# Attention in plain fp32 instead of rounded high and low parts, with scores on 64-row halves and weighted sums on 64-column halves

## The chip, the cores and the metric

The kernel runs on one core of one Trainium2 chip. The metric is the device time of the whole program in microseconds (us), the median of the runs.

## What is computed

The reference is a network of two layers on 4096 tokens (2 sequences of 2048) of 256 features: a Mamba block, a tree of gated feed-forward nodes, an attention, and a feed-forward layer of 64 experts of which each token takes 8. The change touches the attention alone:

```python
q = (hidden_states @ Wq).reshape(b, s, H, D).transpose(0, 2, 1, 3)   # H = 16, D = 64
k = (hidden_states @ Wk).reshape(b, s, HKV, D).transpose(0, 2, 1, 3) # HKV = 4
v = (hidden_states @ Wv).reshape(b, s, HKV, D).transpose(0, 2, 1, 3)
q = _apply_rope(q, cos, sin)
k = _apply_rope(k, cos, sin)
scores = jnp.einsum('bkgqd,bkpd->bkgqp', qg, k) * scale
scores = jnp.where(causal, scores, jnp.float32(-1e+30))
probs = jax.nn.softmax(scores, axis=-1)
out = jnp.einsum('bkgqp,bkpd->bkgqd', probs, v).reshape(b, H, s, D)
return out @ Wo
```

## The kernel before

The stages run one after the other: Mamba (lines 56 on), the tree, the projection with rotation, the attention (lines 1318 to 1793), routing with the output projection, the experts, and the sum. The projection multiplies its plain fp32 weights and inputs at line 1229, for 8 chunks of 512 tokens, 5 pairs, 2 parities and 2 blocks of features: 160 matmuls.

The attention goes through 32 heads (2 sequences of 16). Groups of 4 heads share keys and values, so there are 8 groups. The 2048 queries of a head are 4 bands of 512, each of 4 tiles of 128. A unit is a long and a short band, (3, 0) or (2, 1), and a head is 2 units. In a unit, `CHUNKS` lists 20 score chunks (tile j of band s against keys c of 512 columns; the last chunk of a tile is 1 to 4 blocks of 128 wide, since the attention is causal), and `GROUPS` lists 20 groups (band s against block kb of 128 keys). `STEPS` is 20. One unit's scores are made while the unit before it is turned and summed.

The arithmetic is done in a rounded fp32 format (`F32R`) with high and low parts. `qbuf` holds a query's high part in rows 0 to 63 and its low part in rows 64 to 127; `kbuf` holds the keys' high and low parts, twice over the rows, in two slots for two groups. A score chunk is thus two matmuls over 128 rows (line 1514), and on the diagonal a third adds the mask (line 1518). VectorE takes the maximum (line 1719), ScalarE the exponential (line 1671, bias at line 1732's result). TensorE turns 4 blocks of 128x128 of a group into `ps_t`, which has two banks (line 1527; fewer on the diagonal: 3, 2 and 1). ScalarE copies them as high part (line 1679) and VectorE takes the low part by a subtraction (line 1739). `weigh` (line 1539) multiplies the values, whose high and low columns stand side by side in `vbuf`, with each part: two matmuls into `ps_o`. At a band's end ScalarE copies `ps_o` to `folding` (line 1685), `fold` adds its halves and turns it back, 4 small plain fp32 matmuls (line 1550), and VectorE normalises (line 1757).

TensorE's order is written out by hand: in step v come the scores of the next unit (from step 1 to 17), the turning of group v, and the weighted sum of group v - 2; at a unit's end come the last two sums, the last scores and the fold. `RING` = 5 banks hold scores, `SLOTS` = 4 hold turned groups.

POOL rounds the queries of the next head and makes their low parts (lines 1622, 1624), and once a group does the same for keys (1604, 1606) and values (1612, 1614, 1630). SP issues the loads of queries, keys and values, the stores of the output (line 1494), and the small loads of constants at the start (line 1460); ahead of the first scores TensorE waits for keys and queries.

In the Mamba stage, line 285 sums states (plain fp32, 128 rows), line 277 spreads a row (rounded fp32, 112 rows) and line 265 multiplies with 16 rows (plain fp32). Lines 2112 and 2114, in the routing, multiply plain fp32 with 64 rows.

## Time and profile before

| | us |
|---|---|
| median of 3 runs | 4915.38 |
| lowest and highest run | 4910.9, 4915.8 |
| span of the profiled execution | 4914.1 |
| of it TensorE busy | 4375.7 |

The page gives no time of the profiled execution beside its span; 4914.1 us lies within the three runs, 1.3 us under their median. "Busy" is the union of an engine's instructions. Matmuls are recorded with modelled ends that reach over the start of the next one, so the busy time of a matmul is more than what it takes from the engine; the distance between starts is not subject to this. PE is the matmul side of TensorE, PEld its weight load. A releaser behind an arrow is the instruction that ended a wait.

### The profile page before, as it was taken

To read this page: it belongs to the slowest core of one execution; us is meant where nothing else is said; L and a number is where in the kernel's file an instruction comes from. 1 tells how busy PE (TensorE), PEld (TensorE's weight loads), DVE (VectorE), ACT (ScalarE), POOL (GpSimd) and SP (SyncE) were. 2 spreads that over 40 slices of the span, in tenths; PEclk is the share of its full clock that TensorE was granted. 3 is DMA by queue.
4 is the path that set the end of the run, shared out by engine and by line. 5 is a ranking of instruction groups with operands and counts; after the bars stand their busy time and mean duration, and the time that the engine had idled before them with its cause. 6 is when DMAs were issued, how large, how long until landed. Compare 5 with 4: busy or idle time off the path is not lost. (4 is left out here: it accounts for less than half of the span.)

```text
span 4914.1 us, 82249 instructions
## 1 busy us (share of the span) xinstructions
PE 4375.7 (89%) x20280; PEld 3077.8 (63%) x20311; DVE 3433.2 (70%) x7334; ACT 2814.4 (57%) x6629; POOL 1757.2 (36%) x1411
## 2 busy tenths in 40 slices
PE   7888888789999979999999999999966549999996
PEld 3333333356666568888888888888855437777775
DVE  7999999934434878888888888888844443333336
ACT  7777777522221068888888888888833224444441
POOL 5989989700100021212121221212135553333330
PEclk8999999999999989999999999999987769999999
DMA  1000000021102530202112021202044425554548
GB/s 44 13 13 13 13 27 9 9 87 57 47 17 82 178 102 26 53 26 52 42 44 53 26 52 28 58 26 53 26 155 143 143 97 155 155 157 152 157 138 344
DMA packets 305965, 377.40 MB, mean 77 GB/s; under 512 B 123200, under 2 KB 236608, under 8 KB 300240
## 3 DMA queue, kind: packets, MB, share of 16 engines
q1 hardware_dynamic: 232784, 257.37, 17.3%
q0 software_dynamic: 26112, 73.44, 4.2%
q10 hardware_dynamic: 46944, 45.16, 3.4%
q8 instruction: 50, 0.82, 0.1%
q14 instruction: 75, 0.61, 0.0%
HBM read 223.07 MB, written 152.76 MB: 76 GB/s over the span
## 5 line engine op out<-in xcount | busy, mean ns | idle before, releaser
L1739 DVE TENSOR_TENSOR probsT<-ps_t,probsT 128x512 fp32r<-128x512 f32 (+3 forms) x1280 | 779.5, 609 | 137.8 <-ACT probsT L1679 116.2
L1679 ACT ACTIVATE probsT<-ps_t 128x512 fp32r<-128x512 f32 (+3 forms) x1280 | 686.6, 536 | 256.1 <-PE ps_t L1527 231.3
L1671 ACT ACTIVATE probs<-ps_s,negm 128x512 f32<-128x512 f32 (+3 forms) x1297 | 812.5, 627 | 28.1 <-DVE negm L1732 27.1
L1539 PE MATMUL ps_o<-probsT,vbuf 128*128 128x512 f32 (+3 forms) x2560 | 815.8, 402 | 6.8 <-ACT folding L1685 6.3
L1514 PE MATMUL ps_s<-kbuf,qbuf 128*128 (+1 forms) x2602 | 768.7, 380 | 57.8 <-ACT probs L1671 31.5
L1719 DVE TENSOR_REDUCE pmax<-ps_s 128x1 f32<-128x512 f32 (+3 forms) x1301 | 777.6, 600 | 47.3 <-PE ps_s L1514 23.0
L1527 PE MATMUL ps_t<-idn,probs 128*128 128x128 f32 x4352 | 694.8, 275 | 13.8 <-DVE probsT L1739 13.8
L527 POOL TENSOR_TENSOR dBx<-u,b_all 128x1024 f32<-128x1024 f32 x255 | 612.4, 2414 | 96.5 <-DVE h L623 66.8
L1527 PEld LDWEIGHTS ps_t<-idn,probs 128*128 128x128 f32 x4352 | 517.3, 141 | 135.3 <-DVE probsT L1739 40.9
L1514 PEld LDWEIGHTS ps_s<-kbuf,qbuf 128*128 128x128 f32 x2602 | 445.3, 189 | 177.9 <-issue 63.9
L1622 POOL CAST qbuf<-room_a 128x512 fp32r<-128x512 f32 x132 | 83.1, 630 | 1264.6 <-DMA room_a<-q_scr 754.1
L285 PE MATMUL ps_y<-hc,idn 128*128 128x512 f32 x1024 | 500.5, 612 | 31.3 <-POOL hc L535 29.7
L428 ACT ACTIVATE ps_a<-delta,neg_a 128x512 f32<-128x512 f32 x512 | 350.8, 690 | 226.7 <-DVE h L623 225.3
L623 DVE TENSOR_TENSOR_SCAN h<-ps_a,h_in,dBx 128x512 f32<-128x512 f32 x384 | 469.3, 1266 | 0.9 <-POOL hc L535 0.7
L2588 POOL DMA_INDIRECT y<-y,place x288 | 276.7, 961 | 490.4 <-DVE y L2625 476.4
L2497 PE MATMUL ps_gu<-room_a,xT 128*128 x1160 | 423.3, 488 | 0.3 <-ACT xT L2550 0.3
L1539 PEld LDWEIGHTS ps_o<-probsT,vbuf 128*128 128x128 f32 x2560 | 392.3, 191 | 34.3 <-ACT folding L1685 22.0
L2621 DVE TENSOR_TENSOR hid<-ps_gu,sg 128x192 f32<-128x192 f32 x290 | 103.7, 358 | 402.6 <-ACT sg L2554 374.3
L285 PEld LDWEIGHTS ps_y<-hc,idn 128*128 128x128 f32 x1024 | 197.4, 195 | 216.3 <-issue 153.4
L2190 POOL DMA_INDIRECT xs<-xe,dest x256 | 246.8, 964 | 206.6 <-issue 206.3
L2511 PE MATMUL ps_y<-room_a,hT 96*128 x1152 | 296.4, 379 | 0.0
L632 DVE TENSOR_TENSOR hc<-h,ps_c 128x1024 f32<-128x1024 f32 x224 | 273.3, 1220 | 23.3 <-PE ps_c L277 5.6
(275 smaller groups left out, 6982.7 us busy)
## 6 DMA issues: line engine op xcount, KB each, us to landing
room_b<-xs ACTq DMA_DIRECT2D x294, 136.0 KB
room_a<-q_scr SPq DMA_DIRECT2D x528, 64.0 KB
room_c<-y SPq DMA_DIRECT2D x32, 1024.0 KB, 8.2
room_a<-W_guT SPq DMA_DIRECT2D x64, 384.0 KB
q_scr<-rot SPq DMA_DIRECT2D x64, 256.0 KB, 2.9
attn<-ostage SPq DMA_DIRECT2D x128, 128.0 KB
at<-attn SPq DMA_DIRECT2D x32, 512.0 KB
room_a<-W_downT SPq DMA_DIRECT2D x64, 192.0 KB
```

The costliest lines, as they stand in the source:

```text
L285: last = nc.tensor.matmul(ps_y[:, i, :], idn[:, :], hc[:, q % 2, i, :], start=n == 0, stop=n == NST - 1)
L428: nc.scalar.activation(ps_a[:, s % RING, :], delta[:, c % 2, d, :], ACT.Exp, scale=neg_a[:, d, n:n + 1]).then_inc(dA_ready.sem, 1)
L527: nc.gpsimd.tensor_tensor(dBx[:, q % DRIVES, :, :], u[:, hv * DH:(hv + 1) * DH, :], b_all[:, n:n + 1, :].to_broadcast((P, DH, TC)), ALU.mu ...
L623: nc.vector.tensor_tensor_scan(h[:, q % 2, i, :], ps_a[:, s % RING, :], dBx[:, q % DRIVES, i, :], 0.0 if first else h_in[:, n, d:d + 1], A ...
L1514: last = nc.tensor.matmul(ps_s[:, u % RING, 0:w], qbuf[:, BAND * s + j, :], kbuf[:, bass.ds(kslot, 1), part, c * CW:c * CW + w], start=par ...
L1527: last = nc.tensor.transpose(ps_t[:, t % 2, j * P:(j + 1) * P], probs[:, k, place(k, s, j, kb), :], idn[:, :])
L1539: last = nc.tensor.matmul(ps_o[:, lo:], vbuf[:, kb, :, :], probsT[:, g % SLOTS, part, lo:], start=kb == 0 and part == 0, stop=kb == BAND * ...
L1671: nc.scalar.activation(probs[:, k, at:at + n, :], ps_s[:, u % RING, 0:n * P], ACT.Exp, bias=negm[:, tile, :], accum_out=sums[:, s, j, c:c ...
L1679: nc.scalar.activation(probsT[:, g % SLOTS, 0, lo:], ps_t[:, t % 2, lo:], ACT.Copy).then_inc(high_t.sem, 1)
L1719: nc.vector.reduce_max(pmax[:, tile, c:c + 1], ps_s[:, u % RING, 0:blocks(s, j, c) * P], axis=mybir.AxisListType.X).then_inc(cmax.sem, 1)
L1739: nc.vector.tensor_tensor(probsT[:, g % SLOTS, 1, lo:], ps_t[:, t % 2, lo:], probsT[:, g % SLOTS, 0, lo:].bitcast(F32), ALU.subtract).then ...
L2497: last = nc.tensor.matmul(ps_gu[:, b, 0:2 * FF], xT[:, b, k, :], w_gu[:, bass.ds(e % WSLOTS, 1), k, :], start=k == 0, stop=k == KD - 1)
```

## The change

The operands `qbuf`, `kbuf`, `vbuf` and `probsT` become plain fp32 with no parts. `kbuf` has one slot instead of two, and POOL fills it chunk by chunk at a group's end, each chunk after its last use by the old group. Both row halves of `qbuf` and `kbuf` hold the same 64 rows; a score chunk is one matmul that uses rows 0 to 63 or 64 to 127 in turn, and the mask is added by two bf16 matmuls on the same rows. A weighted sum is one matmul whose 64 output columns go to the lower or the upper half of `ps_o` by the parity of kb; where kb = 1 doesn't cover the first columns, a matmul with zeros fills them. The sums are issued in pairs in every odd step. The turned groups are copied once, by ScalarE in even and by VectorE in odd steps (`by_act`), and the semaphore `t_out` is split into one for each engine. `SLOTS` is 5.

```diff
-    SLOTS = 4
+    SLOTS = 5
...
-    LAG = 2
...
+    K_USED = [max(k * STEPS + v + 1 for k in range(NU) for v, (s, j, chunk_no) in enumerate(CHUNKS[k]) if chunk_no == c) for c in range(BANDS)]
+    K_ORDER = sorted(range(BANDS), key=lambda c: K_USED[c])
...
+    def by_act(g):
+
+        return g % 2 == 0
...
-        idn_r = sb("idn_r", [P, P], F32R)
         idn_2 = sb("idn_2", [P, HD])
-        mask = sb("mask", [P, P])
-        mask_r = sb("mask_r", [P, P], F32R)
-
-        qbuf = sb("qbuf", [P, QT, P], F32R)
-        kbuf = sb("kbuf", [P, 2, 2, LENGTH], F32R)
-        vnext = sb("vnext", [P, QT, 2, HD], F32R)
-        vbuf = sb("vbuf", [P, QT, 2, HD], F32R)
+        halves = sb("halves", [P, 2, P])
+        mask = sb("mask", [P, 2, P])
+        halves_b = sb("halves_b", [P, 2, P], BF16)
+        mask_b = sb("mask_b", [P, 2, P], BF16)
+        nothing = sb("nothing", [P, HD])
+
+        qbuf = sb("qbuf", [P, QT, P])
+        kbuf = sb("kbuf", [P, LENGTH])
+        vbuf = sb("vbuf", [P, QT, HD])
         probs = sb("probs", [P, NU, BLOCKS, P])
-        probsT = sb("probsT", [P, SLOTS, 2, CW], F32R)
...
         @block.tensor
         def _(pe):
-            def scores(hx, kslot, k, v):
+            def scores(hx, k, v):
                 s, j, c = CHUNKS[k][v]
                 u = k * STEPS + v
                 w = blocks(s, j, c) * P
+                rows = slice(HD * (u % 2), HD * (u % 2 + 1))
                 pe.wait_ge(exp_done.sem, exp_done.at(hx, u - RING + 1))
-                for part in range(2):
-                    last = nc.tensor.matmul(ps_s[:, u % RING, 0:w], qbuf[:, BAND * s + j, :],
-                                            kbuf[:, bass.ds(kslot, 1), part, c * CW:c * CW + w],
-                                            start=part == 0, stop=part == 1 and c < s)
+                last = nc.tensor.matmul(ps_s[:, u % RING, 0:w], qbuf[rows, BAND * s + j, :],
+                                        kbuf[rows, c * CW:c * CW + w], start=True, stop=c < s)
                 if c == s:
-                    last = nc.tensor.matmul(ps_s[:, u % RING, w - P:w], idn_r[:, :], mask_r[:, :], start=False, stop=True)
+                    for part in range(2):
+                        last = nc.tensor.matmul(ps_s[:, u % RING, w - P:w], halves_b[rows, part, :], mask_b[rows, part, :],
+                                                start=False, stop=part == 1)
                 last.then_inc(s_done.sem, 1)
 
             def turn(hx, k, g):
                 s, kb = GROUPS[k][g]
                 t = use(k, g)
                 pe.wait_ge(exp_done.sem, exp_done.at(hx, band_end(k, s)))
-                pe.wait_ge(t_out.sem, t_out.at(hx, t - 1))
+                bank_free(pe, hx, t)
                 for j in range(max(0, kb - BAND * s), BAND):
                     last = nc.tensor.transpose(ps_t[:, t % 2, j * P:(j + 1) * P], probs[:, k, place(k, s, j, kb), :], idn[:, :])
                 last.then_inc(t_done.sem, 1)
...
             def weigh(hx, group, k, g):
                 s, kb = GROUPS[k][g]
                 lo = max(0, kb - BAND * s) * P
-                pe.wait_ge(t_out.sem, t_out.at(hx, use(k, g) + 1))
+                rows = slice(HD * (kb % 2), HD * (kb % 2 + 1))
+                taken(pe, hx, use(k, g))
                 if kb == 0:
                     pe.wait_ge(o_ev.sem, o_ev.at(hx, 2 * k + (s == UNITS[k][1])))
                 if kb % BAND == 0:
                     pe.wait_ge(v_set.sem, v_set.at(group, V_ORDER.index(kb // BAND) + 1))
-                for part in range(2):
-                    last = nc.tensor.matmul(ps_o[:, lo:], vbuf[:, kb, :, :],
-                                            probsT[:, g % SLOTS, part, lo:],
-                                            start=kb == 0 and part == 0, stop=kb == BAND * s + BAND - 1 and part == 1)
-                last.then_inc(pv_done.sem, 1)
+                if kb == 1 and lo:
+                    nc.tensor.matmul(ps_o[rows, 0:lo], nothing[:, :], probsT[:, g % SLOTS, lo:2 * lo], start=True, stop=False)
+                nc.tensor.matmul(ps_o[rows, lo:], vbuf[:, kb, :], probsT[:, g % SLOTS, lo:],
+                                 start=kb == 0 or kb == 1 and not lo, stop=kb >= BAND * s + BAND - 2).then_inc(pv_done.sem, 1)
 
             def fold(hx, k, short):
 
                 t = fold_use(k, short)
                 pe.wait_ge(o_ev.sem, o_ev.at(hx, 2 * k + short + 1))
-                pe.wait_ge(t_out.sem, t_out.at(hx, t - 1))
+                bank_free(pe, hx, t)
                 for j in range(BAND):
                     last = nc.tensor.matmul(ps_t[:, t % 2, j * HD:(j + 1) * HD], folding[:, j * P:(j + 1) * P], idn_2[:, :],
                                             start=True, stop=True)
                 last.then_inc(f_done.sem, 1)
 
             pe.wait_ge(rounded.sem, 2)
+            pe.wait_ge(nothing_set.sem, 1)
             s_done.credit(pe)
             t_done.credit(pe)
             pv_done.credit(pe)
             f_done.credit(pe)
-            pe.wait_ge(k_ready.sem, 1)
+            pe.wait_ge(k_ready.sem, BANDS)
             pe.wait_ge(q_ready.sem, 2)
             for v in range(LEAD + 1):
                 if v == STEPS:
                     pe.wait_ge(q_ready.sem, BANDS)
-                scores(0, 0, *chunk(0, v, 0)[1:])
+                scores(0, *chunk(0, v, 0)[1:])
             with pe.Fori(0, NHEADS) as hx:
                 group = pe.snap(hx // GROUP)
-                slot = pe.snap(group % 2)
-                slot_next = pe.snap(((hx + 1) // GROUP) % 2)
+                group_next = pe.snap((hx + 1) // GROUP)
                 for k in range(NU):
                     def next_scores(v):
                         heads, unit, number = chunk(k, v, LEAD)
                         if number == 0 and unit == 0:
                             pe.wait_ge(q_ready.sem, q_ready.at(hx + 1, 2))
-                            pe.wait_ge(k_ready.sem, (hx + 1) // GROUP + 1)
                         elif number == 0:
                             pe.wait_ge(q_ready.sem, q_ready.at(hx + heads, 4))
-                        scores(hx + heads, slot_next if heads else slot, unit, number)
+                        if heads and unit == 0 and number < BANDS:
+                            pe.wait_ge(k_ready.sem, k_ready.at(group_next, K_ORDER.index(number) + 1))
+                        scores(hx + heads, unit, number)
 
                     for v in range(STEPS):
                         if 0 < v < LATE:
                             next_scores(v)
                         turn(hx, k, v)
-                        if v >= LAG:
-                            weigh(hx, group, k, v - LAG)
+                        if v % 2 and v > 1:
+                            weigh(hx, group, k, v - 3)
+                            weigh(hx, group, k, v - 2)
                         if v == FOLD[k]:
                             fold(hx, k, 0)
+                    next_scores(LATE)
+                    next_scores(LATE + 1)
                     weigh(hx, group, k, STEPS - 2)
-                    next_scores(LATE)
                     weigh(hx, group, k, STEPS - 1)
-                    for v in range(LATE + 1, STEPS + 1):
-                        next_scores(v)
+                    next_scores(STEPS)
                     fold(hx, k, 1)
...
+            def set_keys(g, c):
+
+                nc.gpsimd.tensor_copy(kbuf[:, c * CW:(c + 1) * CW], kstage[:, c * CW:(c + 1) * CW]).then_inc(k_ready.sem, 1)
...
             def queries(hx, n):
-                j, low = QUEUE[n], slice(HD, P)
-                tiles = slice(BAND * j, BAND * (j + 1))
-                after(q_ld[j].sem, q_ld[j].at(hx))
-                nc.gpsimd.tensor_copy(qbuf[:, tiles, :], qstage[:, tiles, :]).then_inc(high_q.sem, 1)
-                after(high_q.sem, high_q.at(hx, n + 1))
-                nc.gpsimd.tensor_tensor(qbuf[low, tiles, :], qstage[low, tiles, :], qbuf[low, tiles, :].bitcast(F32),
-                                        ALU.subtract).then_inc(q_ready.sem, 1)
-                after(q_ready.sem, q_ready.at(hx, n + 1))
+                tiles = slice(BAND * QUEUE[n], BAND * (QUEUE[n] + 1))
+                after(q_ld[QUEUE[n]].sem, q_ld[QUEUE[n]].at(hx))
+                nc.gpsimd.tensor_copy(qbuf[:, tiles, :], qstage[:, tiles, :]).then_inc(q_ready.sem, 1)
 
             def set_values(g, n):
                 b = slice(BAND * V_ORDER[n], BAND * (V_ORDER[n] + 1))
-                nc.gpsimd.tensor_copy(vbuf[:, b, :, :], vnext[:, b, :, :].bitcast(F32)).then_inc(v_set.sem, 1)
+                nc.gpsimd.tensor_copy(vbuf[:, b, :], vstage[:, b, :]).then_inc(v_set.sem, 1)
...
             with pool.Fori(0, NGROUPS) as g:
-                head_queries(g * GROUP)
-                keys(g + 1)
-                after(v_set.sem, v_set.at(g))
-                values(g + 1)
-                with pool.Fori(1, GROUP) as j4:
+                with pool.Fori(0, GROUP - 1) as j4:
                     head_queries(pool.snap(g * GROUP + j4))
-
+                head = pool.snap(g * GROUP + GROUP - 1)
+                after(s_done.sem, s_done.at(head, STEPS))
+                for n in range(2):
+                    queries(head + 1, n)
+                after(k_ld.sem, k_ld.at(g + 1))
+                for c in K_ORDER:
+                    after(s_done.sem, s_done.at(head, K_USED[c]))
+                    set_keys(g + 1, c)
+                for n in range(2, BANDS):
+                    queries(head + 1, n)
+
+                after(v_ld.sem, v_ld.at(g + 1))
                 for n, used in enumerate(V_USED):
                     after(pv_done.sem, pv_done.at(g * GROUP + GROUP - 1, used))
                     set_values(g + 1, n)
...
-            def high(hx, k, g):
+            def take_turned(hx, k, g):
                 s, kb = GROUPS[k][g]
                 t, lo = use(k, g), max(0, kb - BAND * s) * P
                 act.wait_ge(t_done.sem, t_done.at(hx, k * STEPS + g + 1))
                 act.wait_ge(pv_done.sem, pv_done.at(hx, k * STEPS + g - SLOTS + 1))
-                nc.scalar.activation(probsT[:, g % SLOTS, 0, lo:], ps_t[:, t % 2, lo:], ACT.Copy).then_inc(high_t.sem, 1)
+                nc.scalar.activation(probsT[:, g % SLOTS, lo:], ps_t[:, t % 2, lo:], ACT.Copy).then_inc(act_out.sem, 1)
...
+            nc.scalar.activation(kbuf[:, :], kstage, ACT.Copy).then_inc(k_ready.sem, BANDS)
...
-            for dst, src in ((idn_r, idn), (mask_r, mask)):
-                nc.scalar.activation(dst[:, :], src[:, :], ACT.Copy).then_inc(rounded.sem, 1)
+            for dst, src in ((halves_b, halves), (mask_b, mask)):
+                nc.scalar.activation(dst[:, :, :], src[:, :, :], ACT.Copy).then_inc(rounded.sem, 1)
...
-                        high(hx, k, v)
+                        if by_act(v):
+                            take_turned(hx, k, v)
...
-            def low(hx, k, g):
+            def take_turned(hx, k, g):
                 s, kb = GROUPS[k][g]
                 t, lo = use(k, g), max(0, kb - BAND * s) * P
-                dve.wait_ge(high_t.sem, high_t.at(hx, k * STEPS + g + 1))
-                nc.vector.tensor_tensor(probsT[:, g % SLOTS, 1, lo:], ps_t[:, t % 2, lo:],
-                                        probsT[:, g % SLOTS, 0, lo:].bitcast(F32), ALU.subtract).then_inc(t_out.sem, 1)
+                dve.wait_ge(t_done.sem, t_done.at(hx, k * STEPS + g + 1))
+                dve.wait_ge(pv_done.sem, pv_done.at(hx, k * STEPS + g - SLOTS + 1))
+                nc.vector.tensor_copy(probsT[:, g % SLOTS, lo:], ps_t[:, t % 2, lo:]).then_inc(dve_out.sem, 1)
```
The rest of the diff allocates and waits on the semaphores (`act_out`, `dve_out`, `nothing_set`), splits the loads of `mask` and `ident` into halves (7 small loads at line 1460 instead of 4), and makes `ACT_TAKES` and `DVE_TAKES`, the counts of copies up to each turn.

## Rows read from the trace of the kernel before

**Rows 1.** The page, part 1: busy us (share of the span) and instructions.
```profile
PE 4375.7 (89%) x20280; PEld 3077.8 (63%) x20311; DVE 3433.2 (70%) x7334; ACT 2814.4 (57%) x6629; POOL 1757.2 (36%) x1411
```
**Rows 2.** The attention as one window; each engine's busy us (instructions), granted clock, DMA.
```profile
1770.00:3574.00 1804.00, 1752.08 (x11010) 1460.59 (x11010) 1562.31 (x3457) 1493.02 (x3970) 343.09 (x320) 1.00 0.16 39
```
**Rows 3.** Waits of PE from 1790 to 3600: us in total, times, longest.
```profile
PE ps_s L1514 <- ACT probs L1671: 26.4, 63, 0.4
PE ps_t L1527 <- DVE probsT L1739: 13.8, 64, 0.3
...
PE ps_o L1539 <- ACT folding L1685: 6.3, 32, 0.2
```
**Rows 4.** Timeline of POOL, one copy a head: start us, us, engine, line, operation.
```profile
2304.79 0.62 POOL L1622 CAST qbuf<-room_a 128x512 fp32r<-128x512 f32 x1 [16.71 <-PE ps_s L1518]
...
2361.16 0.62 POOL L1622 CAST qbuf<-room_a 128x512 fp32r<-128x512 f32 x1 [16.76 <-PE ps_s L1518]
...
2417.48 0.62 POOL L1622 CAST qbuf<-room_a 128x512 fp32r<-128x512 f32 x1 [16.67 <-PE ps_s L1518]
```
**Rows 5.** Timeline of PE inside one head, start us and us first.
```profile
2404.42 0.63 PE L1514 MATMUL ps_s<-kbuf,qbuf 128*128 x2
2404.89 0.22 PE L1518 MATMUL ps_s<-mask_r,idn_r 128*128 128x128 f32 x1
2404.95 0.60 PE L1527 MATMUL ps_t<-idn,probs 128*128 128x128 f32 x4
...
2414.20 1.10 PE L1550 MATMUL ps_t<-idn,folding 128*128 128x64 f32 x8
2415.14 0.28 PE L1527 MATMUL ps_t<-idn,probs 128*128 128x128 f32 x1
...
2423.05 0.62 PE L1514 MATMUL ps_s<-kbuf,qbuf 128*128 x2
...
2423.86 0.71 PE L1539 MATMUL ps_o<-probsT,vbuf 128*128 128x512 f32 x2
2424.41 0.62 PE L1514 MATMUL ps_s<-kbuf,qbuf 128*128 x2
2424.87 0.60 PE L1527 MATMUL ps_t<-idn,probs 128*128 128x128 f32 x4
2425.23 0.71 PE L1539 MATMUL ps_o<-probsT,vbuf 128*128 128x512 f32 x2
```
**Rows 6.** Timeline of PE in the projection, plain fp32.
```profile
1645.10 17.33 PE L1229 MATMUL ps_qk<-room_b 128*128 128x512 f32 x40
1662.27 3.62 PE L1235 MATMUL ps_v<-room_b 128*128 128x256 f32 x16
```
**Rows 7.** 64-row matmuls in the routing (PE), and the clock there.
```profile
4020.77 1.32 PE L2112 MATMUL ps_o<-past,n_b 64*128 64x336 f32 x2
4021.89 1.32 PE L2114 MATMUL ps_g<-own,c_b 64*128 64x336 f32 x2
...
4010.00:4030.00 20.00, 7.00 (x18) 4.09 (x18) 15.28 (x72) 0.00 (x0) 14.00 (x15) 0.50 0.26 91
```
**Rows 8.** Timeline of PE in the Mamba stage, around a matmul with 16 rows.
```profile
607.71 1.88 PE L285 MATMUL ps_y<-hc,idn 128*128 128x512 f32 x4
609.52 1.12 PE L265 MATMUL ps_f<-dt_in,w_dt 16*128 16x512 f32 x2
610.57 0.50 PE L277 MATMUL ps_c<-dbc,sel 112*128 112x512 f32 x1
610.91 1.88 PE L285 MATMUL ps_y<-hc,idn 128*128 128x512 f32 x4
```
**Rows 9.** The weight loads (PEld): there, and in a step of the attention.
```profile
608.14 0.19 PEld L285 LDWEIGHTS ps_y<-hc,idn 128*128 128x128 f32 x1 [0.24 <-issue]
608.57 0.19 PEld L285 LDWEIGHTS ps_y<-hc,idn 128*128 128x128 f32 x1 [0.24 <-issue]
609.52 0.29 PEld L265 LDWEIGHTS ps_f<-dt_in,w_dt 16*128 16x128 f32 x2 [0.76 <-issue]
610.57 0.19 PEld L277 LDWEIGHTS ps_c<-dbc,sel 112*128 112x128 f32 x1 [0.76 <-issue]
...
2423.28 0.59 PEld L1527 LDWEIGHTS ps_t<-idn,probs 128*128 128x128 f32 x4
```
**Rows 10.** The page, part 5: VectorE's subtraction and ScalarE's copy of turned blocks.
```profile
L1739 DVE TENSOR_TENSOR probsT<-ps_t,probsT 128x512 fp32r<-128x512 f32 (+3 forms) x1280 | 779.5, 609 | 137.8 <-ACT probsT L1679 116.2
L1679 ACT ACTIVATE probsT<-ps_t 128x512 fp32r<-128x512 f32 (+3 forms) x1280 | 686.6, 536 | 256.1 <-PE ps_t L1527 231.3
```
**Rows 11.** POOL's groups between 1770 and 3574 us: busy us, mean ns, idle before.
```profile
L1624 POOL TENSOR_TENSOR qbuf<-room_a,qbuf 64x512 fp32r<-64x512 f32 x128 | 164.8, 1287 | 23.0 <-POOL qbuf L1622 23.0
L1622 POOL CAST qbuf<-room_a 128x512 fp32r<-128x512 f32 x128 | 78.9, 617 | 1264.0 <-DMA room_a<-q_scr 754.1 <-PE ps_s L1518 493.6 <-POOL qbuf L1624 16.3
```
**Rows 12.** Timeline at the start of the attention: SP's small loads, TensorE's first score.
```profile
1744.44 0.43 SPq L1460 DMA_DIRECT2D mask<-causal  x1
...
1744.92 1.19 SPq L1460 DMA_DIRECT2D idn<-ident  x2
...
1749.41 3.22 PE L1514 MATMUL ps_s<-kbuf,qbuf 128*128 128x512 f32 x8 [21.66 <-POOL qbuf L1624]
```

More of the change, by code:

```diff
@@ L1352, in attention @@
     NGROUPS = BATCH * KV
-    assert STEPS % RING == 0 and STEPS % SLOTS == 0 and TURNS % 2 == 0
+    assert STEPS % RING == 0 and STEPS % SLOTS == 0 and TURNS % 2 == 0 and STEPS % 2 == 0
     attn_view = attn.rearrange("(n p) d -> p n d", p=P)
@@ L1372, in fold_use @@
         return k * TURNS + (TURNS - 1 if short else FOLD[k] + 1)
+    def by_act(g):
+        return g % 2 == 0
+    ACT_TAKES = [0]
+    DVE_TAKES = [0]
+    for k in range(NU):
+        for t in range(TURNS):
+            folds = t in (FOLD[k] + 1, TURNS - 1)
+            g = t - (t > FOLD[k] + 1)
+            ACT_TAKES.append(ACT_TAKES[-1] + int(not folds and by_act(g)))
+            DVE_TAKES.append(DVE_TAKES[-1] + int(folds or not by_act(g)))
     def chunk(k, v, lead):
@@ L1420, in attention @@
         rounded = tally("rounded")
-        high_k = tally("high_k")
-        k_ready = tally("k_ready")
-        high_v = tally("high_v")
-        v_ready = tally("v_ready")
+        nothing_set = tally("nothing_set")
+        k_ready = tally("k_ready", BANDS)
         v_set = tally("v_set", BANDS)
-        high_q = tally("high_q", BANDS)
         q_ready = tally("q_ready", BANDS)
@@ L1434, in attention @@
         exp_done = tally("exp_done", PER, 1)
-        high_t = tally("high_t", PER)
         o_ev = tally("o_ev", 2 * NU, 1)
-        t_out = tally("t_out", NU * TURNS, 1)
+        act_out = tally("act_out", ACT_TAKES[-1], 1)
+        dve_out = tally("dve_out", DVE_TAKES[-1], 1)
         cmax = tally("cmax", PER)
@@ L1442, in attention, with taken, bank_free @@
         o_out = [tally("o_out%d" % s, 16, 1) for s in range(BANDS)]
-        NCONST = 4
+        NCONST = 7
+        def taken(eng, hx, t):
+            if ACT_TAKES[t + 1] > ACT_TAKES[t]:
+                eng.wait_ge(act_out.sem, act_out.at(hx, ACT_TAKES[t + 1]))
+            else:
+                eng.wait_ge(dve_out.sem, dve_out.at(hx, DVE_TAKES[t + 1]))
+        def bank_free(eng, hx, t):
+            if t >= 2:
+                taken(eng, hx, t - 2)
+            else:
+                taken(eng, hx - 1, NU * TURNS + t - 2)
         def band_end(k, s):
@@ L1457, in _ @@
         def _(sp):
-            for dst, src in ((idn[:, :], ident), (mask[:, :], causal), (idn_2[0:HD, :], ident[0:HD, 0:HD]),
-                             (idn_2[HD:P, :], ident[0:HD, 0:HD])):
-                sp.dma_start(dst, src).then_inc(consts.sem, 16)
+            sp.dma_start(idn[:, :], ident).then_inc(consts.sem, 16)
+            sp.dma_start(idn_2[0:HD, :], ident[0:HD, 0:HD]).then_inc(consts.sem, 16)
+            sp.dma_start(idn_2[HD:P, :], ident[0:HD, 0:HD]).then_inc(consts.sem, 16)
+            sp.dma_start(halves[0:HD, :, :], ident.rearrange("(o r) n -> r o n", r=HD)).then_inc(consts.sem, 16)
+            sp.dma_start(halves[HD:P, :, :], ident.rearrange("(o r) n -> r o n", r=HD)).then_inc(consts.sem, 16)
+            sp.dma_start(mask[0:HD, :, :], causal.rearrange("(o r) n -> r o n", r=HD)).then_inc(consts.sem, 16)
+            sp.dma_start(mask[HD:P, :, :], causal.rearrange("(o r) n -> r o n", r=HD)).then_inc(consts.sem, 16)
             route_first_loads(sp, route_front, Wo, ident)
@@ L1477, in _ @@
                              blank[:, :, :].to_broadcast((P, EXTRA // P, ROW))).then_inc(blanked.sem, 16)
-                sp.wait_ge(v_ready.sem, v_ready.at(g))
+                sp.wait_ge(v_set.sem, v_set.at(g))
                 sp.sem_inc(sp_seen.sem)
@@ L1492, in _ @@
                         for short, s in enumerate(UNITS[k]):
-                            sp.wait_ge(t_out.sem, t_out.at(hx, fold_use(k, short) + 1))
+                            taken(sp, hx, fold_use(k, short))
                             sp.dma_start(attn_view[:, bass.ds(first[s], BAND), bass.ds(col, HD)],
@@ L1500, in _ @@
             sp.wait_ge(k_ready.sem, k_ready.at(NGROUPS))
-            sp.wait_ge(v_ready.sem, v_ready.at(NGROUPS))
+            sp.wait_ge(v_set.sem, v_set.at(NGROUPS))
             sp.wait_ge(k_ld.sem, k_ld.at(NGROUPS))
@@ L1638, in _ @@
             nc.gpsimd.memset(blank[:, :, :], 0.0).then_inc(blank_set.sem, 1)
+            nc.gpsimd.memset(nothing[:, :], 0.0).then_inc(nothing_set.sem, 1)
             for n in range(2):
                 queries(0, n)
-            values(0)
+            after(v_ld.sem, v_ld.at(0))
             for n in range(BANDS):
@@ L1778, in _ @@
                             settle(*ahead(v))
-                        low(hx, k, v)
+                        if not by_act(v):
+                            take_turned(hx, k, v)
                         if v in (BAND, BAND + 1):
```

25 lines of the change are left out of this document (4 added, 21 removed).

## The prediction

> **What bounds the kernel now.** I first read the busy shares [rows 1]: TensorE stands at 89% of the span. The change touches only the attention, so the next view is the stretch from its first to its last transposition, 1770 to 3574 us [rows 2]: 1752 of 1804 us on TensorE, VectorE 1562, ScalarE 1493, granted clock 1.00, which is the 2.4 GHz level. The kernel there is bound by TensorE. The waits say the same [rows 3]: TensorE loses 26.4 us to the exponentials, 13.8 to the low parts and 6.3 to the copy of the output, 46.5 us in all, or 1.5 us for each of 32 heads. One head lasts 56.35 us: the same copy of queries comes at 2304.79, 2361.16 and 2417.48 [rows 4].
>
> Busy time can't price a matmul here, since each is recorded with its pipeline's tail and overlaps the next; I price by starts [rows 5]. A full step is a weighted sum W (2423.86), a score S (2424.41), the turning T of four blocks (2424.87) and again W (2425.23): W 0.55, S 0.46, T 0.36, sum 1.37 us. There are 40 steps a head. T of three, two and one block takes 0.27, 0.14 and 0.05 us. A mask adds 0.07 (score with mask at 2404.42, T at 2404.95: 0.53 against 0.46). A fold takes 0.94 (2414.20 to 2415.14).
>
> **The head, split.** Each unit of 20 steps has 68 blocks to turn, and the 2 units give 28 T of four and four of each shorter kind: 28 x 0.36 + 4 x (0.27 + 0.14 + 0.05) = 11.9 us. Four folds are 3.8, 16 masks 1.1, idle 1.5. The rest of 56.35, 38.0 us, is S and W: 1.01 us for each of what would be 34 full steps (17408 columns of scores, 17408 of sums, over 512) is 34.3, and the narrow ones carry the remainder.
>
> **S and W in plain fp32.** Their price stands in the projection before the attention, which multiplies plain fp32 [rows 6]: 40 records of 512 columns fill 1645.10 to 1662.27, 0.429 us each, and the code's 160 matmuls give 320 records, two for each. So a plain fp32 matmul of 512 columns costs 0.858 us, where the two rounded ones that it replaces cost 0.46 (S) or 0.55 (W). Does a tile of 64 rows make this cheaper? The only 64-row matmuls of the trace are four late ones [rows 7]: two records of 336 columns from 4020.77 to 4021.89, 0.56 us each, at a granted clock of 0.50, the 1.2 GHz level. 672 ticks of 1.2 GHz are 0.56 us: two ticks a column, just as 0.429 us is two ticks a column at 2.4 GHz. Fewer rows save nothing. The new S and W are then 34 x 2 x 0.858 = 58.3 us a head.
>
> T and folds are unchanged: 11.9 + 3.8. The mask becomes two bf16 matmuls: at 0.07 each, 2.2 us. The matmul with zeros comes once a head at 128 columns, 0.2. Idle kept at 1.5. **Bare head: 77.9 us**, 21.6 more than now.
>
> **Switches of the array's shape.** The new S uses 64 rows, W 64 columns, T all of it. In the old attention all three use the full array. A single place of the trace mixes shapes [rows 8]: at 609.52 two records with 16 rows stand between full ones. From 607.71 to 610.91 lie four records, the two, and one rounded matmul: 3.20 us. Six records at 0.429 are 2.57, the rounded one 0.23 (half of S): 0.40 too much for one way in and one way out. The weight loads show how: those of full shape run under the matmul before them, while the load for 16 rows starts at 609.52, when the previous matmul ends, and the next full load at 610.57 [rows 9]. The array empties, and the load stands bare. I take 0.2 us a switch. The bounds are 0 (64-row tiles might not empty it) and 0.2; nothing suggests more.
>
> Here the Trainium skill, TensorEngine Tiling (Array Packing), Key Properties, says that changing the tiling mode drains TensorE. By this rule the row's 0.40 us is the normal case and not an accident of semaphores, and the sum keeps its switches; without it the sum would be the smaller one given under the second rival.
>
> Counting in the new order: steps 1 to 17 of a unit have S between T (2 switches), 8 of them also W behind T (1 more), 42; step 18 leaves W, 1; the end is T-W-S-W-S-fold, 5. That is 48 a unit, 96 a head: 19.2 us. The 20 entries into W load only 64 columns, about 0.05 less each: 18.2 us.
>
> **Pairs on two halves.** Two W now stand side by side on different columns. No row of before shows two matmuls at once in different parts of the array, so this is bounded by 0 and by the whole of one of the pair, 14.6 us a head. Starts follow the program in every row. If that holds, the second record of the first W can run beside the first record of the second, and no more: of 4 record times one is saved. I take this, 58.3/2/4 = 7.3 us, and 0.7 for the two pairs of neighbouring S at the units' ends.
>
> **Head after:** 77.9 + 18.2 - 8.0 = 88.1 us, 31.75 more than 56.35. Times 32: +1016 us.
>
> **What costs nothing.** ScalarE keeps only every other copy of turned blocks: per head 1493/32 - 21.5/2 = 36 us. VectorE loses its subtraction (780/32 = 24.4 us) and takes the other copies, taken at the subtraction's price, half of it [rows 10]: 48.8 - 24.4 + 12.2 = 36.6. Both fall far below the head, so nothing of theirs binds. TensorE covered them already, so halving them gives nothing back. POOL's low parts of the queries, 1.29 us each, lay beside TensorE as well: TensorE's waits name POOL nowhere [rows 3, 11]. Even under the quickest rival below (48.7 us a head) TensorE stays above both.
> The single key buffer is new: at a group's end (8 times) POOL may copy a chunk only after its last score, 0.62 us a copy. The first chunk is released one score before the end; behind it TensorE has a score (0.86) and two narrow W (0.4 and 0.2), which hide it. Cost 0; if the cover fails, 8 x 0.9 = 7 us. Behind that wait on POOL stand the other key chunks, two query copies and the values; the queries are needed a unit later, the first values three steps into the next head, over 4 us on. Queues: SP issues three more small loads at the start, about 1.5 us by its neighbours, while POOL's low parts of the queries, the last thing that the first scores wait for, drop out [rows 12]: 0 net. The opening scores are dearer, 21 x 0.4 us at worst, partly under the exponentials: +5.
>
> Sum: 1016 + 5 = +1021 on the profiled span of 4914.1, so 5935. The median, 4915.4, lies 1.3 us above it: 5936 us. The rivals' times hold the same 5 and 1.3.
>
> **Rivals.** (1) *Switches, but no overlap of the W pairs*: 96.1 us a head, +1272: 6192. For it: nothing in the trace has two matmuls at once. (2) *No emptying between shapes*, so 96 switches are free: 69.9 us a head with the half overlap, +434: 5354; without overlap 77.9, +690: 5610. For it: the 16-row matmul has a smaller tile than 64 rows, and its neighbours wait on semaphores too. Against it: T, S and W wait on semaphores in every step and still load ahead: the loads of T start at 2423.28, while S is under way from 2423.05 to 2423.67.
> (3) *Whole pairs overlap.* Both W run at once, saving 14.6, and both neighbouring S, 1.4: with switches 80.1 us a head, +760: 5680; without, 61.9, +178: 5098. Against it are the starts in program order, with two records per matmul.
> The Trainium skill, TensorE: Matmul & The Clock Gate, Measured speedup vs the span model, has matmuls on separate tiles last hardly longer than one; its measurements, however, are not of a matmul that comes as two records. This is the rule by which rival 3 would win. No run here shows it.
> (4) *Faster.* A plain fp32 record on a 64-wide tile takes one tick a column instead of two, since half the array is free to hold the other half of the product, and no switch empties it. Then S and W are 29.2 us and the head 48.7, 7.65 less than now: -245, and with the opening 4675. It decides where S, W and switches together fall under 56.35 - 19.6 = 36.7 us a head; at one tick a column but with switches (18.2) it is still slower. Against it stand the 0.56 us records.
> (5) *The clock falls* to its lower level because half the array is idle: S and W alone add 58 us a head, to some 7800 us. Against: the clock is 1.00 throughout with TensorE 97% busy, and it would stay above 90% busy [rows 2].
> That the change doesn't do what it says, for instance that the halves are never neighbours, is half true by reading: between two S there is always T, save at a unit's end, so alternating rows earns only the 0.7 us above.
>
> **Numbers.** Forecast 0.40; rival 1 0.20; rival 2 0.22; rival 3 with switches 0.08, without 0.05; rival 4 0.03; rival 5 0.02. The range runs from just under rival 2 to just over rival 1, 5300 to 6220: left out are 0.05 + 0.03 + 0.02 = 0.10, and I grant as much to sizes beyond it. About 0.2% is what a measurement of this kernel can tell from no change. Faster: 0.03 and a little for a mixed case, 0.04. Same 0.01, slower 0.95.
>
> **What would show it.** In the profile after: plain records of S and W at 0.43 us from start to start, two for each of 1280 and 1280; the clock at 1.00; the head near 88 us. For the switches: weight loads of S and T that start only as the matmul before them ends, T taking 0.45 rather than 0.36 up to the next start. For the overlap: the second W starting 0.43 us before the first one's last record is over, a pair lasting 1.29 us and not 1.72 (none) or 0.86 (whole). VectorE and ScalarE near 40% of the stretch. The prediction is wrong if an S on 64 rows takes less than 0.8 us, if the load of T runs under S, or if TensorE shows waits of more than 2 us a head.

## The result and the profile after

The kernel after takes 5685.9 us (median of 4 runs, 5677.4 to 5692.7) against 4915.6: a ratio of 1.157, interval 1.155 to 1.159, 770 us slower. The forecast was 5936 in a range from 5300 to 6220; the time lies in the range, but it is 6 us from the 5680 of rival 3 with switches, which had a chance of 0.08.

The page, with PE's share and three rows of the costliest groups:
```profile
PE 5178.5 (91%) x20894; PEld 2764.5 (49%) x20895; DVE 3134.9 (55%) x6693; ACT 2533.9 (45%) x5989; POOL 1510.8 (27%) x1278
...
L1544 PE MATMUL ps_s<-kbuf,qbuf 64*128 64x512 f32 (+3 forms) x2602 | 1235.8, 585 | 30.7 <-ACT mask_b L1713 23.7
...
L1558 PE MATMUL ps_t<-idn,probs 128*128 128x128 f32 x4352 | 748.4, 289 | 0.0
...
L1572 PE MATMUL ps_o<-probsT,vbuf 128*64 128x512 f32 (+3 forms) x2560 | 637.2, 555 | 0.0
```
Two records for each score (2602, for 1280 scores in the loop and 21 opening ones) and for each sum (2560, for 1280), and only half as much busy time for the sums as for the scores, though both stream the same columns. The attention as one window (columns as in [rows 2]):
```profile
1780.00:4351.00 2571.00, 2552.51 (x11556) 1154.17 (x11555) 1265.48 (x2812) 1211.54 (x3322) 106.83 (x190) 0.99 0.11 28
```
From the first turning (1780.3) to the last (4351.4) it lasts 2571.1 us, 80.35 us a head; before, from 1770.4 to 3570.4, it was 1800.0. That is 771.1 us of the 776.6 between the two spans; the first turning comes 9.9 us later, and the rest of the program is 4.4 us shorter. TensorE is busy 99% of the stretch at full clock; VectorE and ScalarE, at 49% and 47%, bind nothing. TensorE's waits from 1760 to 4330 us (us in total, times, longest us):
```profile
PE ps_t L1581 <- ACT folding L1707: 16.6, 32, 0.5
PE ps_s L1544 <- ACT probs L1693: 5.0, 4, 1.8
PE ps_s L1544 <- POOL kbuf L1635: 1.9, 8, 0.2
```
The waits of [rows 3] have nearly gone, and the single key buffer costs 1.9 us in 8 group changes. The timeline of PE, to be read beside [rows 5]:
```profile
2401.32 1.12 PE L1544 MATMUL ps_s<-kbuf,qbuf 64*128 64x512 f32 x2
2402.37 0.66 PE L1558 MATMUL ps_t<-idn,probs 128*128 128x128 f32 x4
2402.96 1.08 PE L1572 MATMUL ps_o<-probsT,vbuf 128*64 128x512 f32 x4
2403.97 1.12 PE L1544 MATMUL ps_s<-kbuf,qbuf 64*128 64x512 f32 x2
2405.02 0.66 PE L1558 MATMUL ps_t<-idn,probs 128*128 128x128 f32 x4
...
2429.67 1.14 PE L1544 MATMUL ps_s<-kbuf,qbuf 64*128 64x384 f32 x4
2430.42 0.50 PE L1548 MATMUL ps_s<-mask_b,halves_b 64*128 64x128 bf16 x4
2430.85 0.65 PE L1572 MATMUL ps_o<-probsT,vbuf 128*64 128x256 f32 x4
```
A score takes 1.05 us to the next start, four turnings 0.59, and a *pair* of sums 1.01: less than one score. At a unit's end two scores on opposite row halves, with their masks, take 1.18 us together. The weight loads (PEld) of the same step:
```profile
2401.32 0.29 PEld L1544 LDWEIGHTS ps_s<-kbuf,qbuf 64*128 64x128 f32 x2 [0.17 <-issue]
2402.37 0.42 PEld L1558 LDWEIGHTS ps_t<-idn,probs 128*128 128x128 f32 x4 [0.76 <-issue]
2402.96 0.20 PEld L1572 LDWEIGHTS ps_o<-probsT,vbuf 128*64 128x64 f32 x4 [0.17 <-issue]
```
At each change of shape the load starts only about where the matmul before it ends, as [rows 9] had it for the 16-row tile; in the old attention the loads of turning ran under the score. And all four loads of a pair of sums go in within 0.20 us. Which records run together is told by the matmuls of line 1572 that start in the window from 2402.9 to 2403.4, and in the one to 2403.5 (number, then shortest, median, longest in ns, first and last start):
```profile
L1572 PE MATMUL ps_o<-probsT,vbuf x2: 643/643/643, 2403.0 to 2403.0; 128*64 128x512 f32 x2
...
L1572 PE MATMUL ps_o<-probsT,vbuf x4: 592/618/643, 2403.0 to 2403.4; 128*64 128x512 f32 x4
```
Two records start at once, and two more 0.4 us on: the two sums run wholly side by side.

### The profile page after: what moved, and what is told of

It is laid out like the page before. It is cut to its first block and busy times, and to the rows that moved or that the text cites. A ratio compares the mean times of both kernels' runs of the same rounds, so it can differ in the third digit from the quotient of the medians.

```text
span 5690.7 us, 79852 instructions
## 1 busy us (share of the span) xinstructions
PE 5178.5 (91%) x20894; PEld 2764.5 (49%) x20895; DVE 3134.9 (55%) x6693; ACT 2533.9 (45%) x5989; POOL 1510.8 (27%) x1278
## 5 line engine op out<-in xcount | busy, mean ns | idle before, releaser
L1544 PE MATMUL ps_s<-kbuf,qbuf 64*128 64x512 f32 (+3 forms) x2602 | 1235.8, 585 | 30.7 <-ACT mask_b L1713 23.7
L1693 ACT ACTIVATE probs<-ps_s,negm 128x512 f32<-128x512 f32 (+3 forms) x1297 | 796.5, 622 | 108.0 <-DVE negm L1756 108.0
L1701 ACT ACTIVATE probsT<-ps_t 128x512 f32<-128x512 f32 (+1 forms) x640 | 354.9, 555 | 1080.0 <-PE ps_t L1558 1080.0
L1558 PEld LDWEIGHTS ps_t<-idn,probs 128*128 128x128 f32 x4352 | 464.7, 142 | 595.8 <-issue 552.6
L1558 PE MATMUL ps_t<-idn,probs 128*128 128x128 f32 x4352 | 748.4, 289 | 0.0
L1544 PEld LDWEIGHTS ps_s<-kbuf,qbuf 64*128 64x128 f32 x2602 | 369.2, 187 | 565.6 <-ACT probs L1693 287.2
L1572 PE MATMUL ps_o<-probsT,vbuf 128*64 128x512 f32 (+3 forms) x2560 | 637.2, 555 | 0.0
L1640 POOL COPY qbuf<-room_a 128x512 f32<-128x512 f32 x132 | 79.3, 617 | 1971.5 <-DMA room_a<-q_scr 1213.3
L1764 DVE COPY probsT<-ps_t 128x512 f32<-128x512 f32 (+2 forms) x640 | 372.8, 582 | 28.7 <-PE ps_t L1558 25.8
L1693 ACT ACTIVATION_READ_ACCUMULATOR probs<-ps_s,negm 128x1 f32 x1297 | 266.1, 205 | 0.0
```

Of the source, the lines that this page charges most:

```text
L1544: last = nc.tensor.matmul(ps_s[:, u % RING, 0:w], qbuf[rows, BAND * s + j, :], kbuf[rows, c * CW:c * CW + w], start=True, stop=c < s)
L1558: last = nc.tensor.transpose(ps_t[:, t % 2, j * P:(j + 1) * P], probs[:, k, place(k, s, j, kb), :], idn[:, :])
L1572: nc.tensor.matmul(ps_o[rows, lo:], vbuf[:, kb, :], probsT[:, g % SLOTS, lo:], start=kb == 0 or kb == 1 and not lo, stop=kb >= BAND * s + ...
L1693: nc.scalar.activation(probs[:, k, at:at + n, :], ps_s[:, u % RING, 0:n * P], ACT.Exp, bias=negm[:, tile, :], accum_out=sums[:, s, j, c:c ...
L1701: nc.scalar.activation(probsT[:, g % SLOTS, lo:], ps_t[:, t % 2, lo:], ACT.Copy).then_inc(act_out.sem, 1)
L1764: nc.vector.tensor_copy(probsT[:, g % SLOTS, lo:], ps_t[:, t % 2, lo:]).then_inc(dve_out.sem, 1)
```

## The experiments

The theory formed from these rows: pairs on opposite halves overlap wholly, and at a change of shape the next load waits for the matmul before it. With the prices of this profile and of the fourth kernel below, a head is: scores 29.2, sums in pairs 15.5 (a pair lasts as long as its wider sum: 12 pairs of 512 a head, and 4 of 512 and of 256 on the diagonals), turning 15.0, folds 3.8, masks 1.9, zeros 0.2, waits 0.7, less 1.5 for neighbouring scores: 64.8 us. The 15.6 us that are left of 80.35 are put down to the 96 switches, 0.16 each.

The times of the rest of the program differ by chip (the kernel before took 4825.0 and 4821.7 us in the first two sets below, 4917.4 in the last). So the kernels are compared by their attention, from the first to the last turning, over 32; by this measure the kernel before has 56.25 us a head. Kernels 1 to 4 were run once each, on a chip where the kernel before took 90 us less than at first. Their expected whole times start from 5686 us and so stand some 90 us too high there: it is the changes that count. The attention hardly depends on the chip: kernel 7 takes 149.7 us longer than the kernel before on its own chip, and its attention 150.4 us longer than that of the first profile. The kernel after was also run again, beside the last set:

> The kernel after, unchanged, on the chip of the other kernels, so that whole times can be compared: the attention lasts 2571 us from its first to its last turning as in its first profile, within 5 us; the rest of the program may differ by chip. The whole about 5610 us, 49 us less than the one with scores on one row half.

Measured: 5690.1 us (ratio 1.156, 1.154 to 1.158), attention 2571.1 us, as in the first profile (both of these chips have the slower rest). The 5610 us for the whole missed, since on this chip the rest of the program took as long as in the first comparison (before: 4917.4 us).

**1. Both sums of a pair on one half.**
```diff
-                rows = slice(HD * (kb % 2), HD * (kb % 2 + 1))
+                rows = slice(0, HD)
...
-                nc.scalar.activation(folding[:, :], ps_o[:, :], ACT.Copy).then_inc(o_ev.sem, 1)
+                nc.scalar.activation(folding[0:HD, :], ps_o[0:HD, :], ACT.Copy).then_inc(o_ev.sem, 1)
```


> The kernel after, but every weighted sum writes the lower 64 columns; the copy to the folding tile takes 64 partitions and the upper ones stay zero. The shape of the sums and the number of switches stay. Theory (the two sums of a pair run wholly side by side because they lie on different halves): the pair of 512 columns goes from 1.01 us (sums to next scores) to about 1.87 us, 14.6 us a head, 32 heads: +467 us, about 6150 us. Rival (a sum on 64 columns is cheap by itself, two clock ticks fewer a column, and the halves have no part in it): no change, 5686 us. Half overlap, as in the prediction, would have given a pair of 1.44 us in the kernel after, which its trace doesn't show.

Measured: 6025.2 us, attention 2991.8, 93.5 us a head: 13.1 more than after, 14.6 expected. PE's timeline:
```profile
2404.16 1.93 PE L1570 MATMUL ps_o<-probsT,vbuf 128*64 128x512 f32 x4
2406.02 1.12 PE L1544 MATMUL ps_s<-kbuf,qbuf 64*128 64x512 f32 x2
```
The pair takes 1.86 us. Only the half of the second sum has changed, with what belongs to it: the copy to the folding tile, and the zeros of 0.2 us, which are no longer needed. So the overlap comes from the halves, and a 64-column sum alone is as dear as any. The expected 14.6 took half of all sums; a pair of 512 and 384 columns saves only its narrower sum, which makes 13.7. Here both sums also add into the same place in `ps_o`, so this run alone can't part the halves from that; kernel 5 can, for rows.

**2. Scores on all 128 rows.** Query weights are halved and the mask is one matmul, since both row halves hold the same.
```diff
-                last = nc.tensor.matmul(ps_s[:, u % RING, 0:w], qbuf[rows, BAND * s + j, :],
-                                        kbuf[rows, c * CW:c * CW + w], start=True, stop=c < s)
+                last = nc.tensor.matmul(ps_s[:, u % RING, 0:w], qbuf[:, BAND * s + j, :],
+                                        kbuf[:, c * CW:c * CW + w], start=True, stop=c < s)
```


> The kernel after, but scores over all 128 rows (both halves hold the same, the query weights are scaled by half) and the mask in one bf16 matmul. Only the sums still have a shape of their own: 40 switches a head are left of 96. Theory (a switch costs 0.2 us): 56 x 0.2 = 11.2 us less a head, 1 less for the masks, 1.4 more for the lost overlap of neighbouring scores: -10.8 x 32 = -345 us, about 5340 us; turning starts its loads under the scores again, T 0.36 us. Rival (the 0.2 us belongs to the operands or the semaphores, not to the shape): 5690 us, within 50.

Measured: 5332.4 us, 72.0 us a head: 8.4 less than after, where 10.8 were expected. That 5332 is close to the expected 5340 comes from the chip. The rival, which expects no change, falls.
```profile
2402.37 1.12 PE L1541 MATMUL ps_s<-kbuf,qbuf 128*128 128x512 f32 x2
2403.33 0.60 PE L1553 MATMUL ps_t<-idn,probs 128*128 128x128 f32 x4
2403.77 1.02 PE L1541 MATMUL ps_s<-kbuf,qbuf 128*128 128x512 f32 x2
2404.63 0.27 PE L1553 MATMUL ps_t<-idn,probs 128*128 128x128 f32 x1
```
Between two full shapes the score takes 0.86 and the turning 0.44 us, 1.30 together; on 64 rows the same two took 1.05 and 0.59. So the two switches cost 0.34. The turning is not the 0.36 that I expected. At 0.163 us a switch, the 56 switches, the mask and the lost overlap make 9.1 + 0.9 - 1.5 = 8.5 us a head, as measured.

**3. Sums over all 128 columns, the upper 64 of them zeros.**
```diff
-                nc.tensor.matmul(ps_o[rows, lo:], vbuf[:, kb, :], probsT[:, g % SLOTS, lo:],
+                nc.tensor.matmul(ps_o[:, lo:], vbuf[:, kb, :, :], probsT[:, g % SLOTS, lo:],
```


> The kernel after, but sums over all 128 columns, the upper 64 of them zeros. Scores keep their 64 rows. The switches into and out of the sums from turning go (about 20 a head), the overlap goes. Theory: -20 x 0.2 + 14.6 + 0.5 = +11.1 a head, +355 us, about 6040 us. Rival (the overlap doesn't come from the halves): at or under 5600 us.

Measured: 5936.1 us, 90.9 us a head, 10.6 more than after: 11.1 was expected. The rival falls.

**4. Both.**

> Both changes of the two kernels before in one: plain fp32 with no tiles at all. Theory: no switch (-18.2 us a head), no overlap (+14.6 + 1.4), one mask matmul (-1): -3.2 x 32 = -100 us, about 5585 us; the head 77 us, which is the bare sum of the prediction. Were the terms not additive, the time would lie more than 60 us off.

Measured: 5572.0 us, 79.5 us a head (expected 77). The attention is 27 us shorter than after where 100 were expected, so by the mark set above, 60 us, the prices of then don't add up; the nearness of 5572 to 5585 is again the chip's. The rows show which prices were off:
```profile
2400.40 0.61 PE L1553 MATMUL ps_t<-idn,probs 128*128 128x128 f32 x4
2400.84 1.88 PE L1564 MATMUL ps_o<-probsT,vbuf 128*128 128x512 f32 x4
2402.56 0.38 PE L1541 MATMUL ps_s<-kbuf,qbuf 128*128 128x128 f32 x2
```
Sums at 0.86 each, turning at 0.44, no switch. With these prices the terms add up within 0.7 us a head. The 15.6 us of switches were fitted to the kernel after, and the 0.44 of turning was read in kernels 2 and 4; here the sums are held against the other four:

| kernel | terms, us a head | sum | measured |
|---|---|---|---|
| 4, no tiles | 29.2 + 29.2 + 15.0 + 3.8 + 1.0 + 0.6 | 78.8 | 79.5 |
| 3, scores tiled | 78.8 + 0.9 - 1.5 + 76 x 0.163 | 90.6 | 90.9 |
| 2, sums tiled | 64.8 + 1.5 - 0.9 + 40 x 0.163 | 71.9 | 72.0 |
| 1, one column half | 64.8 + 13.7 - 0.2 + 15.6 | 93.9 | 93.5 |

**5. All scores on one row half.**
```diff
-                rows = slice(HD * (u % 2), HD * (u % 2 + 1))
+                rows = slice(0, HD)
```


> The kernel after, but all scores on rows 0 to 63. Theory (alternating rows earn something only where two scores are neighbours: at the two unit ends of a head, 0.86 and 0.64 us, and among the 21 opening scores): +1.5 x 32 = +48 and some 5 for the opening, about 5740 us. Rival (alternating helps in every step, for instance because the load for the other half needs no emptied array): +0.1 us or more in each of 1280 steps, over 5810 us.

Measured: 5663.1 us, ratio 1.174 (1.173 to 1.176), on a chip with a faster rest; attention 2621.2 us, 50.1 more than after (48 expected). At a unit's end the two scores, which lie in different banks, now follow each other:
```profile
2451.68 0.91 PE L1544 MATMUL ps_s<-kbuf,qbuf 64*128 64x384 f32 x2
...
2452.55 1.07 PE L1544 MATMUL ps_s<-kbuf,qbuf 64*128 64x512 f32 x2
...
2453.66 0.65 PE L1572 MATMUL ps_o<-probsT,vbuf 128*64 128x256 f32 x4
```
They take 1.98 us with their masks, 1.18 in the kernel after. Different banks alone give no overlap, the halves do. Alternating the rows earns something only where two scores are neighbours.

**6. Scores in pairs.** Order and nothing else:
```diff
+                    for v in range(1, STEPS, 2):
+                        for g in (v - 1, v):
+                            turn(hx, k, g)
...
+                        if v > 1:
+                            weigh(hx, group, k, v - 3)
+                            weigh(hx, group, k, v - 2)
+                        next_scores(v)
+                        if v < STEPS - 1:
+                            next_scores(v + 1)
```


> The kernel after with its order regrouped: two turnings, two sums, two scores, so that scores are neighbours on opposite row halves in every pair and there are 66 switches a head instead of 96. Theory (pairs of plain fp32 records overlap wholly on rows as on columns): scores 14.6 us a head less, switches 6 less, 1.4 already had: -19.3 x 32 = -618 us, about 5070 us, still above the kernel before. Rival (the ring of 5 score banks can't feed pairs: the second score waits for an exponential): waits of TensorE for the exponentials of 0.3 us a pair or more, 5280 us or above.

Measured: 5604.1 us, ratio 1.162 (1.161 to 1.164), attention 2576.0 us, 80.5 us a head: no gain at all. (The written order has 62 switches a head, not the 66 of the expectation.) PE's timeline:
```profile
2427.04 1.08 PE L1572 MATMUL ps_o<-probsT,vbuf 128*64 128x512 f32 x4
2428.05 1.13 PE L1544 MATMUL ps_s<-kbuf,qbuf 64*128 64x512 f32 x4
2429.11 0.66 PE L1558 MATMUL ps_t<-idn,probs 128*128 128x128 f32 x4
2430.55 0.66 PE L1558 MATMUL ps_t<-idn,probs 128*128 128x128 f32 x4 [0.79 <-DVE probsT L1764]
```
The longest wait of the matmuls in the attention (us in total, times, longest us):
```profile
PE ps_t L1558 <- DVE probsT L1764: 317.9, 478, 1.1
```
Two scores do fit into 1.06 us, so the overlap holds on rows too. But from the first turning of the pair to the second pass 1.44 us, where four turnings behind a switch take 0.59 in the kernel after. Summed from start to start over the whole attention, scores and masks fall by 12.1 us a head against the kernel after, and turning rises by 12.4 (21.1 to 33.5), which eats the gain. Neither theory had named this wait. VectorE takes the maximum of a score first and then copies the turned group that blocks the bank. So it was told to copy first:
```diff
+                        if not by_act(v):
+                            take_turned(hx, k, v)
                         if 0 < v < LATE:
                             peak(*ahead(v))
                             settle(*ahead(v))
-                        if not by_act(v):
-                            take_turned(hx, k, v)
```


> The kernel with paired scores again, but VectorE copies a turned group before it takes the maximum of the same step's scores. The trace of the paired kernel shows TensorE waiting for VectorE's copy, 335 us by the profile, 0.8 us in nearly every pair of steps, since that copy stood behind a maximum. Theory (the wait ate the gain of the pairs; with it gone the pairs and the 62 switches show): head 63 us against 80.5, the attention from first to last turning about 2020 us instead of 2576, the whole about 5050 us. Rival (the ring of 5 score banks is the true limit): the waits move to the exponentials, head above 70 us, 5250 us or more.

Measured: 5314.8 us, ratio 1.080 (1.079 to 1.082), attention 2187.8 us, 68.4 a head: 12.1 less, but 5 short of the theory, between it and its rival. TensorE's timeline:
```profile
2430.32 1.71 PE L1544 MATMUL ps_s<-kbuf,qbuf 64*128 64x512 f32 x4
2431.96 1.09 PE L1558 MATMUL ps_t<-idn,probs 128*128 128x128 f32 x8
...
2437.14 1.21 PE L1544 MATMUL ps_s<-kbuf,qbuf 64*128 64x512 f32 x4
```
The longest wait of its weight loads there:
```profile
PEld ps_s L1544 <- ACT probs L1693: 364.6, 541, 0.9
```
Turning is back at 18.4 us a head. The first score covers the wait of the second, so PE seems busy, but the pair at 2430.32 lasts 1.64 us instead of 1.06: the second score comes late because its bank, one of 5, waits for an exponential. If every group of scores took as little as the quickest one of the same widths in the two paired kernels, the scores would take 3.7 us a head less. Another 1.3 of the missing 5 are 34 switches that the theory counted at 0.2 instead of 0.16. That a larger ring would give the 3.7 back is not shown: none was tried.

**7. Rounded scores, plain sums.** The scores of the kernel before and the sums of the kernel after (an edit of the same operands as in the diff above, for queries and keys the other way round), first in pairs, then in fours with 10 slots:

> Scores, keys and queries as in the kernel before (rounded, high and low parts, 128 rows), sums as in the kernel after (plain fp32, pairs on column halves, one copy of turned blocks). Theory: sums 14.8 us a head and 40 switches, 7 us, against some 20.5 us in the kernel before: +1.3 x 32 = +40, about 4955 us. Rival (the shorter work of ScalarE and VectorE also takes away TensorE's waits of 1.5 us a head): 4900 us.

Measured: 4971.4 us, ratio 1.031 (1.030 to 1.033), 60.95 us a head, 4.7 more than before (1.3 expected). TensorE's waits stay at 50 us, so the rival falls.

> The same with the sums in groups of four and 10 slots for turned groups: 20 switches a head instead of 40. Theory (a switch is 0.2 us and the pairs overlap): 14.8 + 3.5 = 18.3 us of sums a head against 20.5: -70 us, about 4845 us, faster than the kernel before. Rival (the longer lag of the sums makes new waits at the folds): 4915 us or above.

Measured: 5074.7 us, ratio 1.052 (1.051 to 1.054), 64.1 us a head. PE's timeline:
```profile
2423.38 1.94 PE L1570 MATMUL ps_o<-probsT,vbuf 128*64 128x512 f32 x8
2425.24 0.74 PE L1543 MATMUL ps_s<-kbuf,qbuf 128*128 x2
...
2427.85 0.61 PE L1543 MATMUL ps_s<-kbuf,qbuf 128*128 x2 [0.53 <-ACT probs L1692]
```
The longest wait of the matmuls in the attention:
```profile
PE ps_s L1543 <- ACT probs L1692: 158.7, 317, 0.7
```
Four sums take 1.86 us, two pairs and one way in and out, as the theory has it. But the three steps without sums are shorter than an exponential and its read (0.69 + 0.21 us) with the copies beside them, and TensorE waits 158.7 us in place of 26.5. Both versions stay behind the kernel before, so none of these beats it.

## Why the prediction was right, and where it was off

The range held because it was wide, from under rival 2 to over rival 1. Of the steps below, one failed and two terms were mis-sized.

- **What binds, and the price of plain fp32.** Right. Two records for each matmul at 0.43 us, on 64 rows as on 128 (0.86 us a score in kernel 2 and 1.05 with its switches on 64 rows). Rivals 4 and 5 fell; the clock stayed at 0.99.
- **Switches.** The mechanism was right: every load at a change of shape is late, and kernels 2 to 4 remove the cost together with the shapes. The term was mis-sized: 0.163 us on average, not 0.2, so 15.6 us a head and not 18.2. The row behind it [rows 8] holds bare loads of 128 columns on both sides and a rounded matmul whose own share I had to guess. That changing the tiling mode drains TensorE (the Trainium skill, TensorEngine Tiling (Array Packing), Key Properties) agrees with the trace: score and turning are 1.64 us with two switches (64 rows) and 1.30 without (kernel 2).
- **Pairs.** This step failed: "Starts follow the program in every row. If that holds, the second record of the first W can run beside the first record of the second, and no more". The first records of both sums start at 2403.0 and the second ones at 2403.4. The program has one matmul where the trace has two records; I had taken the records for the units of order, and no row of before could tell, since none had two tiles. The saving is 13.7 us a head for the sums (kernel 1: 13.1) and 1.5 for neighbouring scores, not 7.3 and 0.7. The span model of the Trainium skill (TensorE: Matmul & The Clock Gate, Measured speedup vs the span model) agrees with the trace, in plain fp32 too: a pair of sums 1.01 us with its way in and out, one score 1.05.
- **Turning.** Also mis-sized: 0.44 us for four, not 0.36, and 15.0 us a head, not 11.9. Four turnings still show 0.36 ahead of a rounded score in kernel 7, and 0.44 ahead of a plain one in kernel 2. I read this as a recorded start of the rounded matmul that reaches back over the end of the turning, so that in [rows 5] 0.36 charged turning too little and the sums too much; this is argued, not shown. Kernel 7 fits it: there the sums cost, by the prices above, 15.7 with the zeros + 40 x 0.163 = 22.2 us and the head 4.7 more than before, which leaves 17.5 us for the old sums, not 20.5.
- **Sum.** Overlap -7.2, switches -2.6, turning +3.1, waits -0.8, masks -0.3: -7.8 us a head; times 32 that is -250 us, the whole difference between 5936 and 5686. The forecast thus missed by the overlap; its other errors, of up to 3.1 us a head, cancelled to 0.6, and that is luck. The same luck brings rival 3 so near: it had the overlap right, with the same prices of switches and turning.
- **What costs nothing.** Right: no wait for copies of turned groups, 1.9 us for the key buffer. The opening cost 7.5 us in one profile and 7.8 in the other, not 5, if it is taken from the last turning of an earlier stage (line 881, last start at 1554.9 before, 1557.3 and 1551.5 after) to the first of the attention (1770.4, 1780.3 and 1774.8).

## What to carry to other kernels

Plain fp32 in place of a rounded pair of matmuls takes nearly twice the time (a score 0.86 us for 0.46), and tiles of half the array give it back only where two of them are neighbours; here sums got it back and scores didn't. Each change of shape cost some 0.16 us here, so count them in the written order, and group equal shapes as far as banks and the engines that empty them allow. Regrouping moves the wait: before pairing, look at what the other engines do first, and at how many banks are free when the second of the pair comes.

## What was not expected of the hardware

Two plain fp32 matmuls on opposite 64-column halves start their first records together (2403.0) and their second records together (2403.4), with all four weight loads in 0.20 us. On opposite 64-row halves they do the same (2428.1 and 2428.6, kernel 6). A pair takes as long as one: 1.01 us with its way in and out, and 0.85 for each further pair behind it (four sums in 1.86 us, kernel 7 in fours). Two scores of 384 and 512 columns with two masks each took 1.18 us.
